# GpSimd's last residual sum put in front of the scaling of the feed-forward norm in a two-block graph network

## The reference

```python
h = jnp.maximum(_layernorm(x, axis=-1), 0.0)
x = x + _L0_gnn_ref(h, adj, ...)
h = jnp.maximum(_layernorm(x, axis=-1), 0.0)
x = x + _L1_gnn_ref(h, adj, ...)
...
# _L1_gnn_ref, for each of its 3 layers l
    si = x @ attn_w[l, :d]
    sj = x @ attn_w[l, d:]
    scores = si[:, :, None] + sj[:, None, :] + attn_b[l]
    scores = jnp.where(scores >= 0, scores, 0.2 * scores)
    scores = jnp.where(mask, scores, -jnp.inf)
    attn = jax.nn.softmax(scores, axis=-1)
    agg = jnp.einsum('bij,bjd->bid', attn, x)
    h = layernorm(x + agg, g1[l], beta1[l])
    ff = gelu(h @ W1[l] + b1[l]) @ W2[l] + b2[l]
    x = layernorm(h + ff, g2[l], beta2[l])
```

## Time and profile before

| what | value |
|---|---|
| median of three runs | 1618.19 us |
| the profiled execution | 1619.51 us, span 1617.7 us |
| TensorE's mean granted clock | 0.976 |
| TensorE, matmul busy | 1512.0 us, 93% |
| VectorE busy | 1345.7 us, 83% |
| ScalarE busy | 1091.9 us, 67% |
| GpSimd busy | 897.0 us, 55% |

### The profile page before, as it was taken

The page is one execution under the profiler, slowest core; times in us unless marked ns, Lnnn a source line. Parts: engine busy times, 40 slices in busy tenths (PEclk is TensorE's granted clock), DMA queues, the critical chain, the costliest instruction groups (busy, mean ns, idle before and its releaser), DMA issues. The chain is left out here.

```text
span 1617.7 us, 37352 instructions
## 1 busy us (share of the span) xinstructions
PE 1512.0 (93%) x11360; PEld 1272.4 (79%) x11360; DVE 1345.7 (83%) x4302; ACT 1091.9 (67%) x1946; POOL 897.0 (55%) x1008
## 2 busy tenths in 40 slices
PE   6999999369999999989999999899999999999995
PEld 5667777258888888878888888788888888888884
DVE  3899999578898988878988889788989898888952
ACT  1788888236777666657667666667676766767763
POOL 2699998324536456545455464445364655545364
PEclk9999999669999999999999999999999999999998
DMA  6354432510000112110001121100011210000001
GB/s 189 84 155 130 132 127 87 188 51 7 14 8 15 40 30 79 38 35 14 8 14 43 27 82 34 35 15 14 9 45 37 69 48 26 8 14 15 7 27 52
DMA packets 70896, 83.02 MB, mean 51 GB/s; under 512 B 29264, under 2 KB 54096, under 8 KB 70736
## 3 DMA queue, kind: packets, MB, share of 16 engines
q1 hardware_dynamic: 69104, 74.76, 15.8%
q0 software_dynamic: 816, 3.15, 0.7%
q10 hardware_dynamic: 816, 3.15, 0.5%
HBM read 38.95 MB, written 25.17 MB: 40 GB/s over the span
## 5 line engine op out<-in xcount | busy, mean ns | idle before, releaser
L811 ACT ACTIVATE bank<-bank,b_col 128x512 f32<-128x512 f32 x384 | 253.0, 659 | 363.2 <-PE bank L759 363.0
L771 PE MATMUL bank<-w_hi,hid_hi 128*128 128x256 f32 x1536 | 443.1, 288 | 17.5 <-DVE hid_lo L971 13.1
L771 PE MATMUL bank<-w_hi,hid_lo 128*128 128x256 f32 x1536 | 432.8, 282 | 0.0
L771 PE MATMUL bank<-w_lo,hid_hi 128*128 128x256 f32 x1536 | 432.5, 282 | 0.0
L971 DVE TENSOR_TENSOR hid_lo<-bank,hid_hi 128x512 fp32r<-128x512 f32 x384 | 259.3, 685 | 144.7 <-ACT hid_hi L816 141.2
L771 PEld LDWEIGHTS bank<-w_hi,hid_hi 128*128 128x128 f32 x1536 | 289.2, 188 | 53.0 <-DVE hid_lo L971 40.6
L759 PE MATMUL bank<-nT_hi,w_hi 128*128 128x512 f32 x768 | 318.5, 415 | 6.3 <-issue 4.9
L759 PE MATMUL bank<-nT_hi,w_lo 128*128 128x512 f32 x768 | 306.1, 399 | 3.8 <-issue 3.8
L759 PE MATMUL bank<-nT_lo,w_hi 128*128 128x512 f32 x768 | 304.5, 396 | 0.0
L771 PEld LDWEIGHTS bank<-w_lo,hid_hi 128*128 128x128 f32 x1536 | 289.4, 188 | 10.4
L771 PEld LDWEIGHTS bank<-w_hi,hid_lo 128*128 128x128 f32 x1536 | 289.1, 188 | 0.0
(11 more groups left out here) (122 smaller groups left out, 3068.7 us busy)
## 6 DMA issues: line engine op xcount, KB each, us to landing
x_other<-x_cur SPq DMA_DIRECT2D x96, 128.0 KB, 2.4
xin<-in_x_dram SPq DMA_DIRECT2D x16, 512.0 KB, 4.0
first_block_out<-x_res SPq DMA_DIRECT2D x16, 512.0 KB, 2.7
second_block_in<-x_act SPq DMA_DIRECT2D x16, 512.0 KB, 3.7
x_cur<-second_block_in SPq DMA_DIRECT2D x16, 512.0 KB, 3.8
x_fin<-first_block_out SPq DMA_DIRECT2D x16, 512.0 KB, 3.8
out_dram<-x_fin SPq DMA_DIRECT2D x16, 512.0 KB, 2.9
xh_other<-xh SPq DMA_DIRECT2D x128, 33.0 KB, 1.9
```

Of the source, the lines that this page charges most:

```text
L771: mm = pe.matmul(FF[t // 2][:, (t % 2) * D:(t % 2 + 1) * D], a[:, r, t * P:(t + 1) * P], w[:, l, c, :], start=(c == 0 and t % 2 == 0 and p ...
L811: act.activation(h[:], h[:], ACT.Gelu, bias=b1_col[:, l, c:c + 1]).then_inc(s_gelu, 1)
```

## The change

GpSimd's `finish` of slot s-2 is called before `scale_y` of slot s-1 and no longer behind it. No instruction is added or removed, on no other engine does anything move, and in `after` the order stays.

```diff
--- before.py
+++ after.py
@@ -943,10 +943,10 @@
                         U = i * SLOTS + s
                         nxt, nxt2, nxt3 = ahead(s, last)
                         make_base(U, s)
+                        if s > 1:
+                            finish(i, s - 2)
                         if s > 0:
                             scale_y(U - 1)
-                        if s > 1:
-                            finish(i, s - 2)
                         if nxt:
                             scale_n(U + 1)
                         if s > 0:
```

## The result

The changed kernel takes 1646.4 us, the median of five runs (1644.59 to 1649.24), against 1618.88 us of the kernel before (1618.07 to 1621.96, five runs): a ratio of 1.0166, with a 95% interval of 1.0151 to 1.018. It is slower by 27.5 us. The profiled execution took 1646.4 us with a span of 1644.6, 26.9 us more than before. A later set of five runs gave 1645.03 us beside 1619.76, so 25.3 us more.

What follows compares the result with a forecast made beforehand. TensorE, busy 93%, was taken as the bound, with VectorE having no slack at the slot's end. 12 x 1.90 = 22.8 us took the profiled 1619.51 to 1642.3; less 1.3 for the median, 1641.0 us, range 1634 to 1650.

Steps and rivals of the forecast that it cites:

- The mechanism: Before `low` 7, the moved sum's two halves each hold up one VectorE dot product, 1.90 us a slot, delaying TensorE.
- The old place: Behind `scale_y`, the sum slows nothing on VectorE and `scale_n` waits for `ve_a` anyway, so leaving it gives 0.
- dot products three and four: L1014 on VectorE, at 919.09 and 919.56: each meets one half of the sum and takes 1.38 instead of 0.42 us.
- The Trainium skill's rule: At the shared SBUF ports, whichever issues first blocks the other for its whole instruction: 1.29 us a collision, 31 us in all.
- The size: Over twelve slots of laps 0 to 2, 12 x 1.90 = 22.8 us slower; lap 3's two sums cost 0.
- TensorE's clock falls: Rival: longer TensorE waits lower its clock, 3.4 us each; 1651 us with three slots, 1682 with twelve; chance 0.09.
- the main case: Two collisions in each of twelve slots before `low` 7, giving 1641.0 us; chance 0.76.
- Hidden: Rival: GpSimd's 9.57 us of idle time absorb the sum and VectorE isn't hurt, 1618.2 us; chance 0.05.
- One collision: Rival: only one dot product collides before `low` 7 in a slot, 11.4 us in all, 1629.6 us; chance 0.08.
- Both halves without a break, 2.56 us: Upper bound: GpSimd's halves keep the ports between them, VectorE waits 2.56 us a slot, 30.7 us in all, 1648.9 us.
- Faster: Rival: the sum costs nothing and clock falls at the ends of laps 0 and 1 are spared, 1611.4 us; chance 0.02.

Runs made afterwards that it cites:

- the filler: Kernel before plus five extra bn_stats on VectorE ahead of `low` 7 in slots 9 to 12 of laps 0 to 2, no GpSimd move: 1641.23 us, ratio 1.0127.

## Why the prediction was right, point by point

**The mechanism** was right in each step. The old place gave nothing back, and `scale_y` was never late (8.64 us idle before it). The sum met dot products three and four, each in twelve slots and none in lap 3. The forecast gave 2 x 0.95 = 1.90 us to a slot; 1.90 us was measured at `low` 7 and 28.42 - 26.53 = 1.89 us in the slot. TensorE's wait was to be about 2.2 us and is 2.23. What I had assumed without a row, that the first half of the sum takes over the port before the dot product of 919.09, held: there is no gap between `make_base` and the sum.

**The Trainium skill's rule** ("SBUF — State Buffer", section "Who interferes with whom") was weighed against the row at 1.29 us a collision and 31 us in all. Its statement that the other engine waits for the whole instruction is borne out by the sum in one operation, where the dot product lasted until the operation's end. The size went by the row, since the dot product comes when part of the operation has run. What the rule says of instructions with one SBUF input agrees as well, though not in the changed kernel, where the sum is over (930.73) when `low` 7 starts (930.94): in the kernel with four operations `low` 7 takes 0.68 us beside the sum, and 0.69 us without.

**The size** was 22.8 us against 27.5 in the first set and 25.3 in the second, within the range. The term that the sum lacked is the clock's. I had put it in a rival, "TensorE's clock falls", at 3.4 us a time and with a chance of 0.09, and had counted it out for the main case because today's waits never bring it. It did come, in four and three of the twelve slots, about as often as the rival had it ("say three"), but at half a microsecond each; the 3.4 us were read behind a stretch with 4.6 idle us, and are no measure of a dip behind a wait of 2 us. Adding the lengths of all twelve slots in the first profile gives 24.7 us more than before, 1.9 us over 22.8; the two slots behind them in each lap add 0.3 and the start of the second block, by chance, 2.1. That makes 27.1 of the span's 26.9 us. That the dips come with the longer waits for `low` 7 is shown by the filler, which has the waits and the dips without GpSimd's part, and by the runs without such waits, which have none. How a wait turns into a dip in one slot and not in the next stays open.

**The rivals.** Hidden: refuted by the dot products. One collision: not seen in any of the twelve slots. Both halves without a break, 2.56 us: two operations let a dot product through, and only the sum as one operation comes near it, with 2.06 us. Faster: no sign.

## What to carry to other kernels

An engine with idle time is free only if what it does in that time does not share a port with the engine that others wait for. Before moving a GpSimd operation that reads SBUF, list what VectorE does beside the new place and mark the instructions that read two SBUF tiles; the nearest pair that already meets in the trace gives the price, here 0.95 us for an operation of 1.29. Where operations differ in length, go by what is left of GpSimd's operation when VectorE's instruction comes. Where GpSimd has slack, let it wait until VectorE has passed such a stretch: two semaphore waits were worth 2% here, and where it can't wait, short operations cost VectorE less than long ones.

## What the runs showed of the hardware that I had not expected

Matmul waits of 1.75 us (the filler) and 2.03 us (the changed kernel) for `low` 7, in a slot that is otherwise full, come with short dips of TensorE's granted clock, a mean of 0.83 to 0.92 in a window of 10 us, in some slots and not in others of the same shape, and in other slots in another execution. The sum in four operations, with 0.95 us for `low` 7 and at most 1.36 us for the low part behind it, has none, although TensorE was busy for less of the same window (7.92 us, against 8.56 in the filler's):

```profile
660.00:670.00 10.00, 7.92 (x54) 1.00 0.40 129
```

The dips cost 0.5 us each, little beside the 3.4 us that I had read for the falls at the end of a lap.

GpSimd pays for a collision as well, but less. The line of the sum in the changed kernel, to be held against the one in the earlier trace rows (duration min/median/max in ns):

```profile
L904 POOL TENSOR_TENSOR x_fin<-x_fin,y_tok x32: 1259/1444/1477, 602.0 to 1640.0; 128x512 f32<-128x512 f32 x32
```

Its operations went from a median of 1.29 to 1.44 us, since each lets one dot product through. When the sum was one operation it took 2.56 us for 1024 elements, as much as two undisturbed halves, and all of the waiting was VectorE's.
